# All four groups of transposes for the next pass issued ahead of the output projection, instead of two ahead and two inside it

## What is computed

```python
x = src
# attention
n = layernorm(x)
q = (n @ Wq + bq).reshape(B, nb, 64, 8, 128)   # k, v alike
scores = einsum('bnqhd,bnkhd->bhnqk', q, k) * 128 ** -0.5
out = einsum('bhnqk,bnkhd->bnqhd', softmax(scores), v).reshape(B, S, D)
x = x + out @ Wo + bo
# feed-forward
h = square(relu(layernorm(x) @ W_fc.T))
y = h @ W_proj.T
# 5 steps: mem = 0.9 mem + y - (mem > 1);  spikes += (mem > 1)
x = x + spikes / 5
```

## Time and profile before

| what | value |
|---|---|
| median of 2 runs | 1145.9 us (1143.38 and 1148.42) |
| profiled execution, device time | 1142.7 us |
| its span on the slowest core (core 2) | 1141.1 us |
| spans of the 8 cores | 1126.7 to 1141.1 us |
| granted TensorE clock, mean, of the 8 cores | 0.854 to 0.863 |
| TensorE matmul busy | 833.7 us (73%) |

### The profile page before, as it was taken

The page is one execution under the profiler, slowest core; times in us unless marked ns, Lnnn a source line. Parts: engine busy times, 40 slices in busy tenths (PEclk is TensorE's granted clock), DMA queues, the critical chain, the costliest instruction groups (busy, mean ns, idle before and its releaser), DMA issues.

```text
span 1141.1 us, 19208 instructions; the slowest of 8 cores (1126.7 to 1141.1 us)
## 1 busy us (share of the span) xinstructions
PE 833.7 (73%) x6624; PEld 606.0 (53%) x6624; DVE 450.7 (39%) x466; ACT 426.7 (37%) x1097; POOL 266.6 (23%) x128
## 2 busy tenths in 40 slices
PE   0296469845984499566979979798797988979700
PEld 0143334433433344343867868687685877868600
DVE  0104220323123311323018467393754918557282
ACT  3133523252225322412454444444444444444300
POOL 3000100010001100100006235161542616335085
PEclk9997569856995599567998989999998998989955
DMA  9995750077007700553949869497795959969300
GB/s 165 205 232 99 148 112 1 10 139 148 1 1 137 147 13 1 107 136 146 291 163 311 270 194 329 162 329 244 249 330 170 320 188 304 306 199 322 144 0 37
DMA packets 127291, 194.19 MB, mean 170 GB/s; under 512 B 42208, under 2 KB 44256, under 8 KB 127200
## 3 DMA queue, kind: packets, MB, share of 16 engines
q1 hardware_dynamic: 108144, 151.03, 42.9%
q0 software_dynamic: 14448, 33.56, 16.2%
q10 hardware_dynamic: 4608, 8.39, 2.0%
HBM read 192.95 MB, written 25.17 MB: 191 GB/s over the span
## 4 chain that ended last, share of the span: by engine, by line
PE 59%; DMA 19%; ACT 7%; DVE 6%; issue 4%; POOL 3%; SPq 1%; DVEq 0%; ACTq 0%; POOLq 0%
PE psC L824 17%; DMA w2scratch<-w2stage 9%; PE psA L858 9%; PE psB L858 8%; DMA w1slab<-w1scratch 5%; DMA bv_sb<-bv 3%; PE psA L610 3%; PE psA L338 3%; PE psB L610 3%; PE psA L358 2%; PE psB L377 2%; PE psB L338 2%; PE psA L377 2%; PE psB L358 2%; DMA w1scratch<-w2stage 2%
## 5 line engine op out<-in xcount | busy, mean ns | idle before, releaser
L824 PE MATMUL psC<-xn2t_sb,w1slab 128*128 128x256 bf16 x2048 | 276.9, 281 | 15.0 <-ACT xn2t_sb L749 11.7
L824 PEld LDWEIGHTS psC<-xn2t_sb,w1slab 128*128 128x128 bf16 x2048 | 205.0, 101 | 47.1 <-issue 17.9
L835 ACT ACTIVATE h_bf<-psC 128x256 bf16<-128x256 f32 x256 | 97.6, 381 | 221.6 <-PE psC L824 221.4
L858 PE MATMUL psA<-h_bf,w2slab 128*128 128x256 bf16 x1024 | 155.0, 274 | 24.7 <-ACT h_bf L838 22.7
L858 PE MATMUL psB<-h_bf,w2slab 128*128 128x256 bf16 x1024 | 154.2, 273 | 0.0
L912 POOL TENSOR_TENSOR acc_q<-acc_q,spk_q 128x2048 bf16<-128x2048 bf16 x21 | 129.4, 6162 | 62.5 <-DVE spk_q L908 62.5
L917 DVE SCALAR_TENSOR_TENSOR mem_q<-mem_q,y_sb 128x2048 f32<-128x2048 f32 x21 | 125.1, 5959 | 2.2
L858 PEld LDWEIGHTS psA<-h_bf,w2slab 128*128 128x128 bf16 x1024 | 98.5, 98 | 44.7 <-issue 33.2
L838 ACT ACTIVATE h_bf<-h_bf 128x256 bf16<-128x256 bf16 x256 | 106.6, 417 | 24.6 <-ACT h_bf L835 1.5
L219 POOL DMA_DIRECT2D wtmp<-Wfc x32 | 17.0, 533 | 391.1 <-PE psD L502 355.0
L858 PEld LDWEIGHTS psB<-h_bf,w2slab 128*128 128x128 bf16 x1024 | 100.5, 98 | 12.1
(11 more groups left out here) (119 smaller groups left out, 1105.8 us busy)
## 6 DMA issues: line engine op xcount, KB each, us to landing
w2slab<-w2scratch SPq DMA_DIRECT2D x128, 512.0 KB, 6.1
w1slab<-w1scratch SPq DMA_DIRECT2D x128, 512.0 KB, 7.2
x_sb<-x SPq DMA_DIRECT2D x4, 2048.0 KB, 43.0
wtmp<-Wpr POOLq DMA_DIRECT2D x16, 512.0 KB, 7.3
wtmp<-Wfc POOLq DMA_DIRECT2D x32, 256.0 KB, 6.8
w2scratch<-w2stage SPq DMA_DIRECT2D x32, 256.0 KB, 4.7
w1scratch<-w2stage ACTq DMA_DIRECT2D x32, 256.0 KB, 5.1
out<-x_sb POOLq DMA_DIRECT2D x16, 512.0 KB, 8.3
```

Source lines behind the costliest of these rows:

```text
L824: op("pe", lambda E, fc=fc, c=c, hp=hp, s1b=s1b: E.matmul(hp, s1b[:, c * 128:(c + 1) * 128], xn2t_sb[:, c * 256:(c + 1) * 256], start=(c = ...
L835: op("se", lambda E, fc=fc, hp=hp: E.activation(h_bf[fc % 2][:], hp, ACT.Relu), inc="se")
L858: E.matmul(tgt[:, mc * 256:(mc + 1) * 256], slb[:, m * 128:(m + 1) * 128], h_bf[fp % 2][:], start=(fp == 0 and m % 2 == 0), stop=(fp == 31 ...
```

## The change

The groups 2 and 3 are moved on TensorE from behind `jj` 0 and `jj` 1 of the output projection to the place ahead of it, behind groups 0 and 1. Nothing is added or removed; it holds for p = 0, 1 and 2.

```diff
         if p + 1 < PA:
-            xn1t_group(p + 1, 0)
-            xn1t_group(p + 1, 1)
+            for jjx in range(4):
+                xn1t_group(p + 1, jjx)
         wait("pe", "ve", E_attnev[7])
         for jj in range(4):
...
             E_opj = n["pe"]
-            if p + 1 < PA and jj < 2:
-                xn1t_group(p + 1, jj + 2)
             wait("ve", "pe", E_opj)
```

## The result

The changed kernel's median is 1147.6 us (43 runs, 1145.1 us the fastest), against 1145.5 us before (42 runs, 1142.6 us the fastest). The ratio is 1.0020, with a 95% interval of 1.0012 to 1.0028: 2.3 us more, 1.4 to 3.2. (The ratio leaves out the executions in which the cores of a die showed a lower clock; the medians hold them.) That is within 2% and the number is inside the forecast range, but it is clear of zero and nearly three times the 0.8 us of the sum. The question of the experiments is where the other 1.5 us come from.

The account below looks back on a forecast made before the run. TensorE was taken as the limit at the three boundaries between attention passes; 3 x 0.25 = 0.8 us added to the 1145.9 us median gave 1146.7 us, range 1140 to 1153.

Parts of the forecast that it names:

- rival 3: Output projection at each boundary: low clock stays throughout, 12 us each, 36 us for three, 1183 us; chance 0.01.
- rival 1: Boundaries: the hole delays the clock's rise, 4 to 6 us over before, 1150 to 1152 us; chance 0.13.
- Nothing is gained by moving the groups: At the boundaries neither end has a hole to fill; groups 2 and 3 leaving their old places removes 0.91 us.
- The wait that takes their place: Group 2 waits for ScalarE's copy of group 0, starting 2.26 us after group 0; projection starts 2.32 us later than now.
- The covered waits: VectorE's additions stay covered by 2.8 us, ScalarE's last copies finish 16 us before Q, and no DMA is moved.
- The direct cost, 0.25 us: At a boundary, with the clock's rise unmoved, the hole at half clock makes Q start 0.25 us late.
- Does the rise stay?: At each boundary the clock's rise was taken to stay in place despite the hole, costing 0.25 us for all three.
- low bound: Cost of a boundary if the clock's rise is unmoved: 0.25 us, the value taken.
- high bound: Cost of a boundary if the rise moves out: 1.4 us keeping its distance from the projection, 2.1 us at pass 0's distance.
- Rival 2: Boundaries: moved transposes run in time idle anyway, so the projection flows better; gains 2.7 us, 1143.2; chance 0.05.
- Rival 4: The order changes nothing on the chip because the waits end in the same place: 1145.9 us; others' chance 0.01.
- strict reading: Clock gate at a boundary: the hole makes the activity count start again, so each boundary would cost the upper bound.

Follow-up runs that it names:

- no_hole: Changed kernel, but groups 2 and 3 go into psC, so group 2 no longer waits for ScalarE's copy: 21.10 us a boundary, total 0.9995 of before.
- hole_in_old_order: Kernel before, but group 1 uses group 0's half of psD and waits for its copy, nothing moved: 22.81 us a boundary, one time, 1157.3 us.
- three_holes: Changed kernel, but groups 0 to 3 all use psD's first half, each waiting for the previous copy: 26.36 us a boundary, one time, 1162.3 us.

## Why the prediction was right in kind and short in size

The forecast was slower by 0.8 us; it is slower, by 2.3 (1.4 to 3.2). That this lies inside 1140 to 1153 says little, since that range was made from the scatter of two runs and would have held all outcomes but rival 3. The chances were laid out by size: 0.80 for 0 to 1.5 us over before and 0.13 for rival 1 at 4 to 6. The measured 2.3 falls between the two.

- *Nothing is gained by moving the groups.* Right: the old places cost 0.9 us and are gone (162.50, 164.66 and 168.96 stand 2.15 us or twice that apart), and Q waits for nothing in either kernel.
- *The wait that takes their place.* Right, from the earlier trace rows: the second pair 2.26 us behind the first, projection at 3.98 us, 0.40 us idle in front of group 2 at the boundaries read, put down to ScalarE.
- *The covered waits* (VectorE's additions, ScalarE's last copies, no DMA): right, with the 2.8 us of slack that was worked out.
- *The direct cost, 0.25 us.* Right: on core 2 the boundary is 22.09 us; 21.48 + 0.25 and half of the 0.7 us by which its rise is late make 22.08. The text called it the half of a hole of 0.46 us; no_hole shows that the hole is 0.61, half of which is 0.30, and that the 0.06 us added for group 3 is there without a hole as well (1.71 us in place of 1.66). The sum came out right because it took the projection's start, 3.98 us, whole from the earlier trace rows.
- *"Does the rise stay?" is the step that failed.* "I take the low one, 0.25, for all three" should have been 0.63: the hole pushes the rise out by 0.75 us on average, worth 0.38 us a boundary. The reason given for it, that the early rise on core 4 came behind an idle time of 2.47 us, did not bear it: that idle time lies ahead of the first transpose, the hole lies inside the work that lets the clock rise. What the earlier trace rows really show is the edge: a rise 2.7 us behind the start is the earliest of the 24 boundaries of before, and with the hole the whole spread, this edge with it, lies some 0.7 us later. The mean cost lies between the low bound and the high one (1.4 us), a third of the way up. For three boundaries that is 1.9 us in place of 0.8. The row taken from pass 0 for the high bound, a rise 8.8 us behind the first transpose, was that of core 2 alone; in the same profile the clock had risen before Q on cores 0, 4, 6 and 7 (last section).
- *Rival 1* (the hole delays the clock) was thus the mechanism, at a part of its price; 4 to 6 us would have needed a hole of the size of hole_in_old_order (1.75 us a boundary, 5.3 us for three). The sign given for it, rises beyond 5.5 us, could not tell: those of before reach 5.8.
- *Rival 2* (the groups would run in idle time) is out: no_hole gains nothing, though all four groups stand ahead. *Rival 3* (low clock throughout) is out: the latest rise in 48 changed boundaries is 6.5 us behind the start. The Trainium skill's rule that stood beside it ("TensorE: Matmul & The Clock Gate", "A second HAM failure mode: psum-queue depth-cycling") is not borne out by holes of this kind: in no boundary of before, of the changed kernel or of three_holes does a block of the projection behind the second run slow again, so the clock, once up, did not fall. *Rival 4* is out, because the interval excludes 1.

The Trainium skill ("TensorE: Matmul & The Clock Gate", section on the HAM clock gate) says that activity releases the throttle. The strict reading, in which a hole makes the count start again, had been given as the high bound and not taken; the runs show it to hold for the hole of 1.25 us and not for that of 0.40 us.

## What to carry to other kernels

A short wait placed in TensorE's first microseconds after a lull can cost more than its half (0.63 us for one of 0.61, 1.75 for one of 1.41, both counted in lost starting time): look whether the buffers behind a row of transposes alternate fast enough for the engine that empties them, and if not, give the later groups another bank (a PSUM tile that is free at that point), a faster copy, or real matmuls in between. At such a place put first the work whose inputs are ready earliest; here the projection could start 0.9 us before the transposes. When an effect is 0.2% of the time, measure the stretch itself on all cores and repetitions, and work out the clock's share from its length.

## What the runs showed that was not expected

Behind a hole of 1.25 us of TensorE idle time the clock behaved as if the work ahead of it had not been done: the rise came 2.6 to 5.6 us behind the end of one such hole and 2.6 to 5.5 us behind the end of the last of three, where it comes 2.7 to 5.8 us behind the start without any. A hole of 0.40 us did not do that: the rise came 3.3 to 6.5 us behind the start, that is 1.0 to 4.2 us behind the hole's end. It moved the rise by 0.75 us on average (give or take 0.3), about as much as the hole is long.

The two kinds of hole differ in more than length: 8 transposes stand ahead of the long one and 16 ahead of the short one. The start of pass 0 tells the two apart. It is the same in the ten profiles of this case (pair of groups, 0.40 us idle, pair, 1.36 us idle, Q), so there are 80 of it. Core 6 of the kernel before, against core 2 in the earlier trace rows:

```profile
49.03 1.54 PE L304 MATMUL psD<-ident,xn_bf 128*128 128x128 bf16 x16 [0.40 <-ACT xn1t_sb L315]
52.32 3.61 PE L338 MATMUL psA<-xn1t_sb,wq_sb 128*128 128x512 bf16 x16 [1.74 <-ACT xn1t_sb L315]
```

In 27 of the 80 the first 16 matmuls of Q take 3.61 us, as here, so the clock had risen before them. In 21 of these it rose while the second pair ran, which is shown with 1.52 to 1.87 us in place of 1.93; the earliest rise was 3.1 us behind the first transpose, and the idle time behind the pair did not take it back. In the other 53 the 16 matmuls take 4.91 to 6.55 us, so the rise came (4.91 - 3.61) / 0.215 x 0.43 = 2.6 us to 5.9 us behind the end of the idle time, and never within the first 2.6. That is the distance of the boundaries once more, this time behind 32 transposes. So a hole of this length does it behind much work as behind little. (The granted clock reads 1.00 in this stretch of core 2 while 8 matmuls take 3.3 us, the pace of 1.2 GHz; the durations are used.) Between 0.40 and 1.25 us nothing was run, so where one behaviour turns into the other stays open.

The Trainium skill ("TensorE: Matmul & The Clock Gate", section on the HAM clock gate) lets the moment of the rise vary by half a microsecond either way from run to run; in the 24 boundaries of before it varies over 3.1 us (2.7 to 5.8), and here the measurement decides. Also, 0.40 us of idle time in the profile stood for 0.61 us of lost TensorE time, since the length shown for the last transposes ahead of a wait reaches beyond the point where the next could have started: two pairs without a hole start 1.66 us apart, while each is shown 1.86 us long.
